# A three-layer cross-interaction kernel on one core: layer 0 packed, the second block written out, and a new order of the first loads

## What is computed

```python
e = jnp.stack([tbl_0[ids[:, 0]], ..., tbl_38[ids[:, 38]]], axis=1)
x0 = xk = e
for W in [f0, f1, f2]:                     # (39*39,128), (128*39,128), (128*39,128)
    z = jnp.einsum('bfd,bgd->bfgd', x0, xk).reshape(b, f * g, d)
    xk = jnp.einsum('bpd,pm->bmd', z, W)
    outs.append(xk)
z = jnp.sum(jnp.concatenate(outs, axis=1), axis=-1)       # 512 x 384
h = jnp.concatenate([z, dense_ctx], axis=1)               # 512 x 400
h = jnp.maximum(h @ W_top1 + b_top1, 0.0)
h = jnp.maximum(h @ W_top2 + b_top2, 0.0)
y = h @ W_top3
```

## Time and profile before

| | us |
|---|---|
| median of 3 runs | 659.19 (656.44 to 663.04) |
| the profiled execution | 662.05 |
| its span in the profile | 660.1 |
| mean granted clock of TensorE | 0.984 |
| busy: TensorE, VectorE, ScalarE, GpSimd | 629.3, 541.1, 541.4, 480.6 |

### The profile page before, as it was taken

One profiled execution on the slowest core, in us unless ns is written; L12 is line 12 of the kernel. 1 busy time (PEld: TensorE's weight loads), 2 busy tenths in 40 slices (PEclk: granted clock), 3 DMA queues, 4 the chain that ended last, 5 costly groups with the idle time before them and its releaser, 6 DMA issues.

```text
span 660.1 us, 12277 instructions
## 1 busy us (share of the span) xinstructions
PE 629.3 (95%) x2653; PEld 488.4 (74%) x2653; DVE 541.1 (82%) x1224; ACT 541.4 (82%) x1884; POOL 480.6 (73%) x453
## 2 busy tenths in 40 slices
PE   0879899999999999999999999999999999999898
PEld 0467588888888888888888888888888888773673
DVE  0669779898898989898989898989889898996870
ACT  1457679989898989898989898989989898994762
POOL 5888879898988989898989898989878652002330
PEclk9989999999999999999999999999999999996999
DMA  8336522313122232313132213231313303002000
GB/s 217 66 72 128 118 75 44 81 42 81 42 62 61 53 70 45 78 21 89 23 81 42 75 42 81 42 81 42 81 41 68 102 1 97 18 0 77 1 0 1
DMA packets 65502, 40.32 MB, mean 61 GB/s; under 512 B 37486, under 2 KB 50480, under 8 KB 65482
## 3 DMA queue, kind: packets, MB, share of 16 engines
q1 hardware_dynamic: 54201, 35.37, 22.2%
q0 software_dynamic: 5184, 1.29, 2.1%
q10 hardware_dynamic: 6097, 3.44, 2.1%
HBM read 38.13 MB, written 1.94 MB: 61 GB/s over the span
## 4 chain that ended last, share of the span: by engine, by line
PE 89%; DMA 3%; DVE 2%; issue 2%; SPq 1%; ACT 1%; POOL 1%; ACTq 0%; DVEq 0%
PE psa L916 13%; PE psa L912 13%; PE psa L913 13%; PE psd L912 8%; PE psd L916 8%; PE psd L913 8%; PE psg L886 5%; PE ps L850 4%; PE ps L849 4%; PE ps L851 3%; PE psg L976 1%; DMA x_rows_first<-emb_tiles 1%; PE psg L970 1%; PE psg L971 1%; PE psd L991 1%
## 5 line engine op out<-in xcount | busy, mean ns | idle before, releaser
L730 ACT ACTIVATE parts<-psa,x0c 128x128 f32<-128x128 f32 x1536 | 449.1, 457 | 56.4 <-PE psa L916 51.8
L606 DVE SCALAR_TENSOR_TENSOR parts<-psd,x0c,parts 128x128 f32<-128x128 f32 x960 | 265.9, 342 | 54.3 <-PE psd L916 52.4
L577 DVE TENSOR_REDUCE cur<-parts 128x64 f32<-128x1536 f32 x128 | 223.6, 1747 | 6.5 <-DVE parts L606 2.5
L912 PE MATMUL psa<-w1h,x1h 128*128 128x512 f32 x384 | 168.9, 440 | 2.0 <-ACT parts L730 1.5
L413 POOL TENSOR_TENSOR z0l<-pairs,z0h 117x512 fp32r<-117x512 f32 (+1 forms) x98 | 126.8, 1303 | 42.7 <-ACT z0h L683 42.0
L916 PE MATMUL psa<-w1h,x1l 128*128 128x512 f32 x384 | 152.4, 397 | 3.2 <-DVE x1l L567 3.2
L913 PE MATMUL psa<-w1l,x1h 128*128 128x512 f32 x384 | 151.4, 394 | 0.0
L394 POOL DMA_INDIRECT emb<-tables,idx x130 | 126.4, 972 | 24.3 <-issue 24.3
L403 POOL TENSOR_TENSOR pairs<-x0t,pairs 117x512 f32<-117x512 f32 (+1 forms) x98 | 126.7, 1302 | 3.0 <-DMA x0t<-x_rows 2.2
L912 PE MATMUL psd<-w1h,x1h 128*128 128x512 f32 (+1 forms) x256 | 100.9, 394 | 0.6 <-DVE parts L606 0.6
L916 PE MATMUL psd<-w1h,x1l 128*128 128x512 f32 (+1 forms) x256 | 97.6, 381 | 0.0
(11 more groups left out here) (91 smaller groups left out, 574.3 us busy)
## 6 DMA issues: line engine op xcount, KB each, us to landing
pairs<-x_rows SPq DMA_DIRECT2D x105, 156.0 KB
pairs<-x_rows SPq DMA_DIRECT2D x30, 234.0 KB
x0t<-x_rows SPq DMA_DIRECT2D x45, 78.0 KB
gram<-w ACTq DMA_DIRECT2D x3, 832.0 KB, 7.7
emb<-tables,idx POOLq DMA_INDIRECT x130
pairs<-x_rows_first SPq DMA_DIRECT2D x8, 136.5 KB
x_rows<-emb SPq DMA_DIRECT2D x13, 72.0 KB, 2.2
wt_sb<-w_top SPq DMA_DIRECT2D x1, 768.0 KB, 6.1
```

Source lines behind the costliest of these rows:

```text
L577: return dve.tensor_reduce(cur1[:, t % 2, first:end], terms[:, first:end, :, :], AX.XY, ALU.add)
L606: op = dve.scalar_tensor_tensor(acc, y[:, M * j:M * j + M], x0c[:, t, GF * g + j:GF * g + j + 1], acc, ALU.mult, ALU.add)
L730: op = act.activation(lanes(dst, j), y[:, M * j:M * j + M], ACT.Copy, scale=x0c[:, t, GF * g + j:GF * g + j + 1])
L912: pe.matmul(y[:, 0:n], hi, w1h[:, c], start=True, stop=False)
```

## The change

**Layer 0 packed** (from block 2 on): steps 0 to 3 get 11 more rows of pairs each, on partitions 117 to 127 (`XOFF`, `pair_rows`), which take over one of the two shifts of the seventh step. To avoid pairs that stand twice, rows of two other shifts are exchanged (`MOVED`), which splits one load into three. The seventh step (`MIXED`) holds the remaining shift three times over on 117 partitions: the low half is written over the first 39 (`mixed_low_part`), its weights are put together by `w0_mix`, and one matmul does what three did. Packed weights are loaded and added for this (`w0p`), on GpSimd. A block's row loads go from 12 DMAs to 18.

**The second block written out**: block 1 leaves the loop, with order tables of its own. Halves of x1 of block 1 and of the products of block 2, which stood between blocks 0 and 1, move into it. The split of w0 moves from the head to the end of block 0 (ScalarE's high part) and to GpSimd (low part).

**The head**: identity and mask are loaded by SyncE behind the identifiers; ScalarE's weight loads wait for the identifiers to land; the table load of ScalarE is brought ahead of w1's loads. Tiles 2 and 3 are written before tiles 1 and 2 are loaded. The three small tables of the MLP and the packed weights follow on SyncE. The order tables of block 0 are new.

```diff
-L0_AT_FIRST = {(2, 8): [0], (3, 0): [1], (3, 2): [2], (3, 4): [3], (3, 5): [4], (3, 7): [5], (3, 8): [6]}
+L0_AT_FIRST = {(2, 8): [0, 1], (2, 9): [2], (3, 2): [3], (3, 3): [4], (3, 6): [5], (3, 7): [6]}
 TURN_AT = (0, 8)
-TURN_AT_FIRST = (2, 6)
-FIRST_AT = {(0, 6): 1, (1, 0): 2, (1, 6): 3}
-FIRST_HIGH_AT = {(0, 2): 1, (1, 0): 2, (1, 3): 3}
-FIRST_Z0_AT = {(0, 0): 1, (0, 1): 2, (1, 0): 3}
-SECOND_Z0_AT = {(2, 0): [0, 1], (2, 1): [2], (2, 2): [3, 4], (2, 3): [5, 6]}
-FIRST_LOW_AT = {(0, 2): 1, (1, 0): 2, (1, 1): 3}
+TURN_AT_FIRST = (2, 5)
+FIRST_AT = {(0, 6): 1, (1, 0): 2, (1, 7): 3}
+FIRST_HIGH_AT = {(0, 1): 1, (1, 2): 2, (2, 1): 3}
+FIRST_Z0_AT = {(0, 0): 1, (0, 1): 2, (0, 2): 3}
+SECOND_Z0_AT = {(2, 0): [0, 1], (2, 1): [2], (2, 2): [3], (2, 3): [4], (3, 0): [5, 6]}
+FIRST_LOW_AT = {(0, 2): 1, (1, 0): 2, (2, 0): 3}
 TFPC = 16
 TCH = -(-F // TFPC)
 TGATHERS = TILES * TCH
 WARMING = 4
+SECOND_HIGH_AT = {(0, 0): 1, (0, 4): 2, (1, 0): 3}
+SECOND_LOW_AT = {(0, 1): 1, (0, 2): 2, (0, 3): 3}
+SECOND_ZH_AT = {(0, 1): 0, (0, 5): 1, (1, 0): 2, (1, 1): 3, (1, 2): 4, (1, 4): 5, (1, 5): 6}
+L0_AT_SECOND = {(1, 2): [0], (1, 3): [1, 2], (1, 8): [3], (1, 9): [4], (2, 0): [5], (2, 2): [6]}
+W0_MIX_AT = (1, 4)
+W0H_AT_FIRST = (3, 1)
...
 SUM_AT = (2, 0)
-SUM_AT_FIRST = (3, 2)
+SUM_AT_FIRST = (3, 1)
 HIGH_AT = {(2, 3): 0, (3, 1): 1, (3, 4): 2}
-HIGH_AT_FIRST = {(3, 4): 0}
+HIGH_AT_FIRST = {(3, 5): 0}
 LOW_AT = {(2, 3): 0, (3, 1): 1, (3, 3): 2}
-LOW_AT_FIRST = {(3, 3): 0}
+LOW_AT_FIRST = {(3, 2): 0}
 SCALARS_AT = {(2, 3): 0, (3, 1): 1, (3, 2): 2}
-SCALARS_AT_FIRST = {(2, 2): 0, (2, 3): 1, (3, 0): 2}
+SCALARS_AT_FIRST = {(3, 2): 0, (3, 3): 1, (3, 5): 2}
 PIECES = [(0, 2), (2, 4), (4, L0T)]
 LAST = BB * (F - FPC * (CH - 1))
 assert BB * FPC == 128 and SHIFTS % FPC == 0
 SCR_DMAS = 3
 FIRST_WRITES, FIRST_LOADS = 4, 1 + SPT
-PIECE_DMAS = [2 * SPT, SPT, SPT]
+FIRST_PIECE_DMAS = [2 * SPT, SPT, SPT]
+PIECE_DMAS = [2 * SPT + 2, SPT + 3, SPT + 1]
+XF, XN = 10, 128 - ROWS
+XOFF = [18, 21, 29, 32]
+MOVED = {7: (3, 10, 18), 10: (0, 10, 21)}
+MIXED = L0T - 1
+assert XF + XN - 1 + XOFF[-1] < F + SHIFTS
...
+def pair_rows(k):
+    return 128 if k < len(XOFF) else ROWS
...
         graw = gram[:, :, :].rearrange("p f b -> p (f b)")
         w1raw = graw[:, 0:F * M]
+        wt1raw = wt1_sb[:, :, :].rearrange("p k n -> p (k n)")
+        w0p = wt1raw[:, 0:L0T * M]
+        w0pb_raw = wt1raw[:, L0T * M:2 * L0T * M]
...
                 sp.dma_start(rows_at(FPC * (CH - 1), LAST, 1), src[0:LAST, CH - 1:CH, :]).then_inc(scr_written, 16)
                 sp.dma_start(rows_at(F, 128, SHIFTS // FPC), src[:, 0:SHIFTS // FPC, :]).then_inc(scr_written, 16)
+            def load_some(i, k, first, n, f, rows, row, step):
+                src = bass.AP(scr_rows.tensor, row * COLS, [[COLS, rows], [step * COLS, n], [1, COLS]])
+                sp.dma_start(pairs[F * k + f:F * k + f + rows, first:first + n, :], src).then_inc(loaded[i], 16)
+            def load_piece(i, first, end):
+                for k in range(SPT):
+                    s = SPT * first + k
+                    if s in MOVED:
+                        low, high, away = MOVED[s]
+                        also, until, away2 = MOVED[s + SPT]
+                        load_some(i, k, first, 2, high, F - high, high + s, SPT)
+                        load_some(i, k, first, 2, low, high - low, low + away, away2 - away)
+                        load_some(i, k, first, 2, also, low - also, also + s, away2 - s)
+                    else:
+                        load_some(i, k, first, end - first, 0, F, s, SPT)
+                if first < len(XOFF):
+                    src = bass.AP(scr_rows.tensor, (XF + XOFF[first]) * COLS,
+                                  [[COLS, XN], [(XOFF[first + 1] - XOFF[first]) * COLS, 2], [1, COLS]])
+                    sp.dma_start(pairs[ROWS:128, first:first + 2, :], src).then_inc(loaded[i], 16)
+                else:
+                    src = bass.AP(scr_rows.tensor, (SHIFTS - 1) * COLS, [[0, SPT], [COLS, F], [1, COLS]])
+                    sp.dma_start(pairs[0:ROWS, MIXED, :], src).then_inc(loaded[i], 16)
             def load_rows(b):
                 sp.wait_ge(scr_written, 16 * SCR_DMAS * b)
                 for i, (first, end) in enumerate(PIECES):
                     sp.wait_ge(l0_steps, L0T * (b - 1) + end)
-                    for k in range(SPT):
-                        n = min(end, len(range(k, SHIFTS, SPT))) - first
-                        src = bass.AP(scr_rows.tensor, (k + SPT * first) * COLS, [[COLS, F], [SPT * COLS, n], [1, COLS]])
-                        sp.dma_start(pairs[F * k:F * k + F, first:first + n, :], src).then_inc(loaded[i], 16)
+                    if b == 1:
+                        for k in range(SPT):
+                            n = min(end, len(range(k, SHIFTS, SPT))) - first
+                            src = bass.AP(scr_rows.tensor, (k + SPT * first) * COLS, [[COLS, F], [SPT * COLS, n], [1, COLS]])
+                            sp.dma_start(pairs[F * k:F * k + F, first:first + n, :], src).then_inc(loaded[i], 16)
+                    else:
+                        load_piece(i, first, min(end, MIXED))
                     if i == 0:
                         if b == 1:
...
+                        if b > 1:
+                            sp.dma_start(x0t[ROWS:128, :], scr_rows[XF:XF + XN, :]).then_inc(loaded[0], 16)
             def first_rows_to_dram(t):
...
             sp.dma_start(ids_sb[:, :], ids).then_inc(ids_in, 16)
+            sp.dma_start(ident_sb[0:ROWS, :], ident).then_inc(ident_in, 16)
+            sp.dma_start(mask_sb[:, :], mask).then_inc(mask_in, 16)
             first_rows_to_dram(0)
             load_first_rows(0)
-            for t in range(1, TILES):
-                first_rows_to_dram(t)
-                load_first_rows(t)
+            first_rows_to_dram(1)
+            first_rows_to_dram(2)
+            load_first_rows(1)
+            first_rows_to_dram(3)
+            load_first_rows(2)
+            load_first_rows(3)
+            sp.dma_start(bt1_sb[:, :], bt1).then_inc(const_in, 16)
+            sp.dma_start(bt2_sb[:, :], bt2).then_inc(const_in, 16)
+            sp.dma_start(wt3_sb[:, :], wt3).then_inc(const_in, 16)
+            sp.dma_start(w0p.rearrange("p (t m) -> p t m", m=M), w0pa).then_inc(w0p_in, 16)
+            sp.dma_start(w0pb_raw.rearrange("p (t m) -> p t m", m=M), w0pb).then_inc(w0p_in, 16)
             for b in range(1, NBLK):
                 rows_to_dram(b)
                 load_rows(b)
+            sp.wait_ge(w0_mixed, 2)
+            sp.wait_ge(w0l_ready, 1)
...
+                pool.tensor_tensor(low_slot(i), pairs[0:pair_rows(k), k, :], high_slot(i).bitcast(F32),
                                    ALU.subtract).then_inc(z0l_ready, 1)
+            def mixed_low_part(b):
+                pool.wait_ge(z0h_ready, (b - 2) * NS + MIXED + 1)
+                mixed = high_slot(MIXED)[0:F, :]
+                pool.tensor_tensor(mixed, pairs[0:F, MIXED, :], mixed.bitcast(F32), ALU.subtract).then_inc(z0l_ready, 1)
...
+                for c in range(4):
+                    gather_early(1, c)
+                pool.wait_ge(w0p_in, 32)
+                pool.tensor_tensor(w0p, w0p, w0pb_raw, ALU.add).then_inc(w0p_summed, 1)
+                for c in range(4, 7):
                     gather_early(1, c)
                 spread(0, 3)
                 gather_early(1, 7)
+                pool.wait_ge(w0h_ready, 1)
+                pool.tensor_tensor(w0l[:, :], w0p, w0h[:, :].bitcast(F32), ALU.subtract).then_inc(w0l_ready, 1)
                 z0(2, 0)
                 gather_early(1, 8)
...
-                    pair_low_part(b + 1, 6)
+                    mixed_low_part(b + 1)
...
+                        if (t, n) == (0, 0) and not starts(b) and not second(b):
                             low_part(b, TILES - 1)
                         if n == 0 and (t or not starts(b)):
                             finish_second_half((t - 1) % TILES)
+                        if second(b) and (t, n) in SECOND_LOW_AT:
...
             block_of(0, True, slice(BB, 2 * BB))
-            low_part(1, 1)
-            low_part(1, 2)
-            with dve.Fori(1, NBLK - 2) as b:
+            block_of(1, True, slice(2 * BB, 3 * BB))
...
+            def w0_mix():
+                act.wait_ge(w0l_ready, 1)
+                c = slice(M * MIXED, M * MIXED + M)
+                act.activation(w0l[0:64, c], w0p[0:64, c], ACT.Copy).then_inc(w0_mixed, 1)
+                act.activation(w0l[64:2 * F, c], w0p[64:2 * F, c], ACT.Copy).then_inc(w0_mixed, 1)
...
-                        if t == 0 and n == 0 and not starts(b):
+                        if starts(b) and (t, n) == W0H_AT_FIRST:
+                            act.wait_ge(w0p_summed, 1)
+                            act.activation(w0h[:, :], w0p, ACT.Copy).then_inc(w0h_ready, 1)
+                        if second(b) and (t, n) == W0_MIX_AT:
+                            w0_mix()
```

(40 more changed lines are left out.)

75 lines of the change are left out of this document (51 added, 24 removed).

## The result

The changed kernel takes 661.02 us (median of 20 runs, 658.43 to 669.84) against 659.0 us for the kernel before (20 runs, 655.82 to 663.04). The ratio is 1.0042, 95% interval 1.0023 to 1.006: 0.2 to 0.6% slower, which is within 1% of no change. The forecast was 644.8 us, so the 14.4 us that the prediction adds up are missing, and two more. The profiled execution took 668.18 us (span 666.3); since it is one of the longer ones, I show beside it the profile of the same kernel, unaltered, from the first set of experiments ("run again", span 655.9, ratio 1.0026).

What follows compares the result with a forecast made beforehand. TensorE was taken to bound the loop, a chain of transfers the head. Gains of 6.5 + 2.0 + 4.5 + 1.4 = 14.4 us off the 659.19 us median gave 644.8 us; range 638 to 654.

Steps and rivals of the forecast that it cites:

- The packing: Loop, blocks 2 to 15: layer 0 goes from 21 matmuls to 19, saving 6.5 us, or 0 if another engine sets the block.
- Rival 2: Only the head's changes pay, since in the loop ScalarE or VectorE sets the block: 651.3 us, chance 0.05.
- Identifiers first: Head: identifiers land alone, gathers start 2.4 us earlier, block 0 starts 2.0 us earlier (bounds 0.5 and 5.7).
- Writes ahead of loads: Block 0: later tiles' loads go out earlier, TensorE's 3.16 us wait becomes 0.4; gain 4.5 us (bounds 0 and 4.9).
- The second block written out: Block 1: the 1.51 us wait and lower clock go, 2.3 us of GpSimd waits come; gain 1.4 us (bounds -0.2, 3.75).
- Rival 1: Only packing pays; the head's transfers take each other's place, block 1 gives back block 0's gain: 652.7 us, chance 0.14.
- 34.33 and busy throughout: Sign of being right, in the loop: blocks 34.33 us long with TensorE busy throughout.
- Tile 3's load some 9 us earlier: Sign of being right, in block 0: tile 3's load issued some 9 us earlier than 39.04.
- No wait over 1 us in block 0: Sign of being right, in block 0: no wait there lasts over 1 us.
- Block 2 near 104.7: Sign of being right, at block 2's start: near 104.7 us instead of 113.06.
- First layer-1 matmul near 25.5: Sign of being right, at the head's end: first layer-1 matmul near 25.5 us; later than 27 meant wrong.
- rival 4: Slower: GpSimd comes late in every loop block, at the low half of layer-0 step 4; 687 us, chance 0.08.

Runs made afterwards that it cites:

- less step 6: Kernel before, but from block 2 on the seventh layer-0 step makes one matmul instead of three (two products left out): 653.54 us, ratio 0.9967.

## Why the prediction was wrong, point by point

**The packing (6.5 us predicted, 0.3 to 0.6 found).** The price was right: two matmuls are worth 0.47 to 0.495 us a block once their place lets them count, 6.4 us. The step that failed is the one sentence that let it through, that 34.33 stays above ScalarE's 31.67 and VectorE's 30.90. It compares sums over a block. ScalarE's idle time, 2.8 us in 4 waits, lies between tile 0's end and (2,2), where layer 0's steps hold TensorE up; from there ScalarE has none for 22 us. TensorE has two ways round the block, its own list and "its list up to (2,2), then ScalarE's stretch, then the VectorE accumulation that frees (3,9)'s buffer". Before, both were the same length to within some hundredths (less step 6 took two matmuls off the first and left 34.78 of 34.785), and the second didn't show. Packing shortened the part of the first that lies beside the second. Rival 2 named the mechanism in words ("ScalarE or VectorE sets the loop block") and got 0.05 on the strength of the same sums.

**Identifiers first (2.0 predicted, between -0.5 and +0.4 found; against the two other profiles with before's head, -1.1 to 0).** The landing (2.1, taken as 2.4) and the third gather's 6.24 (6.08 to 12.38 in the profile of after) came as written. The term that failed is the 0.4 us by which tile 0's writes would be slowed: with the issue of the last one 5.4 against 1.43 is 4.0. I had argued that the stream is almost over by then. It is not (290 GB/s between 14 and 16 us), since the same step of the change pushes the weights back by 2 us. The upper bound of the earlier trace rows for a write, 3.31, was itself too low: a write in the stream waits longer than any write of before did. The gathers moved out of the stream's way by as much as the writes moved into it; taking the head start back changes the first layer-1 matmul by -0.3 us. The Trainium skill (DMA: Bandwidth & Descriptors, section Queues, rings and completion order) says that a DMA engine takes turns between the queue rows packet by packet. The prediction read this as leaving the gathers nearly free of the weights; the 6.3 us here speak against that reading, as the earlier trace rows did.

**Writes ahead of loads (4.5 predicted).** As a step by itself it held: tile 3's load 6.4 earlier (6.8 predicted), VectorE's wait for tile 2 down from 3.77 to 0.46 (1.93 in the profile of after), TensorE's 3.16 us stand and the lower clock behind it gone, and undoing it costs 0.0041 to 0.0055 of the time, 2.7 to 3.6 us (the ratios are of different sets). What failed is the assumption that the gain is carried on. Block 1's rows are loaded when tile 3's layer 0 is through, 3.1 us earlier (46.50 instead of 49.60), and VectorE's multiplications of those rows then met GpSimd's new passes. At block 1's start 0.6 us is left of all the head's gains in "run again" (73.90 against 74.51), and the other two profiles show a loss.

**The second block written out (1.4 predicted, a loss of 2.3 to 3.8 found).** Here three costs were put at nothing. The two 128x896 passes "stand ahead of 70.2, in the time in which it waited": true for GpSimd, but they block VectorE (one multiplication 2.75 us instead of 0.68), and VectorE's last multiplication is what x0t's load waits for. The second piece's loads stand behind x0t's on SyncE, at 71.27: 3.81 us for GpSimd. I had written that they "stand behind waits for TensorE's steps", and looked at the loop only. And the waits: 1.8 at step 4 and 0.5 at step 5 predicted, 1.3 at step 0 and 2.7 at step 4 found, with the granted clock at 0.78 between 90 and 100 in "run again" (0.83 between 100 and 110 in the profile of after). The lower clock behind the wait was in the lower bound of the term, -0.2, and it came; the loss went beyond that bound. In "run again" the parts add up: 0.6 from the head, -3.75 from block 1 and 0.3 from the loop are 2.8 us late at the last block, 541.22 against 538.41; the ratio of the medians there says 1.7, with an interval of 0.1 to 3.3.

**The range and the rivals.** Range 638 to 654, measured 661.02. Rival 1, "only the packing pays, the head's transfers take each other's place", had the right picture of the head. That the packing pays nothing as well was in no case, though each term had such a bound in the working: 0 for packing, 0.5 for the head start, 0 for the writes, -0.2 for block 1. Even their sum, 0.3 us faster, lies above what came, 2.0 slower, because block 1's loss exceeded its bound. The four terms were treated as if they failed one at a time.

**What the list of signs said.** 19 matmuls a block: yes. 34.33 and busy throughout: no. Identifiers by 3.5: yes (2.8). Tile 3's load some 9 us earlier: 6.4. No wait over 1 us in block 0: no, 1.48 at L958. Block 2 near 104.7: no, 116.2 at the earliest. First layer-1 matmul near 25.5: 28.06, which the prediction had named as a sign of being wrong (later than 27). A wait for GpSimd's low halves behind block 2: none; rival 4 did not come. A granted clock under 1.00 inside the loop: none.

## What to carry to other kernels

Before a busy share is read as room, read where on the timeline an engine's waits lie. If one has none from some group to the end of the loop, only work removed ahead of that group was worth anything here, and the cheapest test is to cut the same small piece of work in two places of the kernel before. A transfer that is moved off another lands on a third: follow the stream's end, and price every transfer in the new window at no less than the slowest row seen inside the stream; here even that row, 3.31, was too low. A pass costed at nothing because its own engine is idle must be looked at for what else its operands' port or queue serves.

## What the hardware showed that I had not expected

- A VectorE multiplication of two SBUF operands, 0.68 us alone, took 2.2 to 3.1 us when a GpSimd pass of 2.1 us over SBUF ran. Apart from it, it took 0.68 again.
- Tile 0's small writes were waited for 5.4 us from the start of the last one's issue beside the weights' stream, 1.97 with a third of the stream put off, 1.87 with the stream started earlier, and 1.43 in the kernel before. Writes of block 1's rows, issued by 40 to 46, were followed by their load 3.1 to 10.3 us later in different runs. In some of these the load also waits for TensorE, but in the profile of after it does not (53.08, layer 0 of tile 3 started at 47.57). What makes a write take 9.5 us there stays open.
- Between 600 and 620 us, where the tail begins, the granted clock was 0.66 over 20 us, some 14 of them at the lower level, in the profiles of before and of after and not in two others of the same program as after: 7 us of time, as much as the whole change was expected to bring in the loop. What sets it off stays open.
